# The three products of two units, woven on TensorE so that neighbours write different PSUM banks

## The reference

```python
# attention, 32 features, no softmax
scores = (xn @ q_w) @ (xn @ k_w).T * decay_weights      # strictly causal
attn = (scores @ (xn @ v_w)) @ o_w.T * out_scale
# four experts, the two best of each token mixed by a softmax of the router's logits
e0 = silu(xn @ sw_w1) * (xn @ sw_w3) @ sw_w2            # 128 -> 512 -> 128
e1 = gelu(sym(xn) @ me_c1w + me_c1b) @ me_c2w + me_c2b  # 128 -> 256 -> 128
h2 = layer_norm(syn + attn_of_syn)                      # linear maps of xn
e2 = layer_norm(h2 + relu(h2 @ f1w + f1b) @ f2w + f2b) @ gen_w + gen_b
e3 = gelu(xn @ ml_w1 + ml_b1) @ ml_w2 + ml_b2           # 128 -> 512 -> 128
```

## Time and profile before

| | |
|---|---|
| median of 3 runs | 501.11 us (500.59 to 501.36) |
| profiled execution | 500.6 us, span 498.8 us |
| PE busy | 484.0 us (97%), 3138 matmuls |
| weight loads busy | 425.3 us (85%) |
| DVE busy | 389.7 us (78%) |
| ACT busy | 224.7 us (45%) |
| POOL busy | 172.3 us (35%) |
| mean granted TensorE clock | 0.997 of full speed |

### The profile page before, as it was taken

The page is one execution under the profiler, slowest core; times in us unless marked ns, Lnnn a source line. Parts: engine busy times, 40 slices in busy tenths (PEclk is TensorE's granted clock), DMA queues, the critical chain, the costliest instruction groups (busy, mean ns, idle before and its releaser), DMA issues.

```text
span 498.8 us, 9722 instructions
## 1 busy us (share of the span) xinstructions
PE 484.0 (97%) x3138; PEld 425.3 (85%) x3138; DVE 389.7 (78%) x1310; ACT 224.7 (45%) x403; POOL 172.3 (35%) x307
## 2 busy tenths in 40 slices
PE   5899999999999999999999999999999999999995
PEld 3779898988989898898989989898898989889894
DVE  4696878779687887868789697878969788795875
ACT  3742717255262734616364361725526272452621
POOL 4642325344142433415243241524324243340320
PEclk9999999999999999999999999999999999999998
DMA  8300010000101001010100101010010100100000
GB/s 259 14 20 4 1 44 1 20 24 1 43 0 42 0 0 42 0 42 0 42 0 0 42 0 42 0 31 11 0 42 0 42 0 2 40 2 22 2 21 21
DMA packets 18497, 11.47 MB, mean 23 GB/s; under 512 B 944, under 2 KB 17840, under 8 KB 18480
## 3 DMA queue, kind: packets, MB, share of 16 engines
q1 hardware_dynamic: 18192, 11.25, 8.5%
q10 hardware_dynamic: 288, 0.01, 0.0%
HBM read 6.80 MB, written 4.19 MB: 22 GB/s over the span
## 4 chain that ended last, share of the span: by engine, by line
PE 94%; DVE 3%; DMA 1%; ACT 1%; issue 1%; POOLq 0%; DVEq 0%; POOL 0%
PE EX L904 23%; PE S L938 12%; PE S L940 11%; PE S L939 11%; PE ATT L997 7%; PE EX L916 6%; PE EX L924 3%; PE S L979 2%; PE S L947 2%; PE TR L865 2%; PE S L949 2%; PE S L948 2%; PE S L1016 2%; PE S L1018 2%; PE S L1017 1%; PE TR L976 1%
## 5 line engine op out<-in xcount | busy, mean ns | idle before, releaser
L938 PE MATMUL S<-xh,WH 128*128 128x512 f32 x224 | 94.1, 420 | 0.0
L940 PE MATMUL S<-xh,WL 128*128 128x512 f32 x224 | 88.3, 394 | 0.0
L939 PE MATMUL S<-xl,WH 128*128 128x512 f32 x224 | 88.3, 394 | 0.0
L904 PEld LDWEIGHTS EX<-W,hid 128*128 128x128 f32 x512 | 59.6, 191 | 1.4
L904 PE MATMUL EX<-scaled,hid 128*128 128x128 f32 x512 | 59.8, 275 | 0.0
L904 PE MATMUL EX<-W,hid 128*128 128x128 f32 x512 | 59.7, 274 | 0.0
L410 POOL TENSOR_TENSOR hidl<-hid,hidh 128x512 fp32r<-128x512 f32 x32 | 40.6, 1292 | 52.9 <-ACT hidh L511 52.9
L904 PEld LDWEIGHTS EX<-scaled,hid 128*128 128x128 f32 x512 | 58.5, 192 | 0.1
L374 POOL TENSOR_TENSOR veps_x<-mv_x,eps 128x4 f32<-128x4 f32 x16 | 3.2, 201 | 156.3 <-DVE mv_x L542 156.3
L652 DVE SCALAR_TENSOR_TENSOR OUT<-EX,coef,OUT 128x128 f32<-128x128 f32 x192 | 53.7, 342 | 1.3 <-PE EX L916 0.2
L938 PEld LDWEIGHTS S<-xh,WH 128*128 128x128 f32 x224 | 42.2, 188 | 14.7 <-DVE gate L728 4.6
(11 more groups left out here) (158 smaller groups left out, 963.5 us busy)
## 6 DMA issues: line engine op xcount, KB each, us to landing
X<-x SPq DMA_DIRECT2D x16, 256.0 KB, 2.9
out<-OUT SPq DMA_DIRECT2D x16, 256.0 KB, 2.4
W<-weights SPq DMA_DIRECT2D x1, 768.0 KB, 8.2
W<-weights SPq DMA_DIRECT2D x1, 512.0 KB, 5.8
W<-weights SPq DMA_DIRECT2D x1, 384.5 KB, 6.8
W<-weights SPq DMA_DIRECT2D x1, 384.0 KB, 6.3
mask<-falling SPq DMA_DIRECT2D x1, 256.0 KB, 11.7
W<-weights SPq DMA_DIRECT2D x1, 192.5 KB, 4.6
```

The lines of the kernel that those rows point to most:

```text
L904: ins = pe.matmul(EX[EX_BANK[e]][:, t, :], hid[e][:, j, t * P:(t + 1) * P], weight[:, j * P:(j + 1) * P], start=(e == 0 and j == 0), stop= ...
L938: pe.matmul(bank[:, :], wh, hi, start=True, stop=False)
L939: pe.matmul(bank[:, :], wh, lo, start=False, stop=False)
L940: pe.matmul(bank[:, :], wl, hi, start=False, stop=True).then_inc(unit_ready, 1)
```

## The change

The helper `three` for one unit is replaced by `pair` for two. It asks for both banks first, then does the six matmuls by turns, one into each bank. Every use of `three` is changed: a and b of each gate, c0 with c1, c2 with c3, f1_0 with f1_1, m0 with m1. The other engines' code is as it was.

```diff
-                def three(name, col, hi, lo):
-
-                    bank = fill(name)
-                    wh, wl = WH[:, col:col + P], WL[:, col:col + P]
-                    pe.matmul(bank[:, :], wh, hi, start=True, stop=False)
-                    pe.matmul(bank[:, :], wh, lo, start=False, stop=False)
-                    pe.matmul(bank[:, :], wl, hi, start=False, stop=True).then_inc(unit_ready, 1)
+                def pair(first_name, first_col, second_name, second_col, hi, lo):
+
+                    one, two = fill(first_name), fill(second_name)
+                    one_h, one_l = WH[:, first_col:first_col + P], WL[:, first_col:first_col + P]
+                    two_h, two_l = WH[:, second_col:second_col + P], WL[:, second_col:second_col + P]
+                    pe.matmul(one[:, :], one_h, hi, start=True, stop=False)
+                    pe.matmul(two[:, :], two_h, hi, start=True, stop=False)
+                    pe.matmul(one[:, :], one_h, lo, start=False, stop=False)
+                    pe.matmul(two[:, :], two_h, lo, start=False, stop=False)
+                    pe.matmul(one[:, :], one_l, hi, start=False, stop=True).then_inc(unit_ready, 1)
+                    pe.matmul(two[:, :], two_l, hi, start=False, stop=True).then_inc(unit_ready, 1)
...
                 def gates(j):
-                    three(f"a{j}", SPLIT["w1"] + j * P, h, l)
-                    three(f"b{j}", SPLIT["w3"] + j * P, h, l)
+                    pair(f"a{j}", SPLIT["w1"] + j * P, f"b{j}", SPLIT["w3"] + j * P, h, l)
...
-                for j in range(4):
-                    three(f"c{j}", SPLIT["ml"] + j * P, h, l)
+                for j in (0, 2):
+                    pair(f"c{j}", SPLIT["ml"] + j * P, f"c{j + 1}", SPLIT["ml"] + (j + 1) * P, h, l)
...
-                three("f1_0", SPLIT["f1"], h2h[:, :], h2l[:, :])
-                three("f1_1", SPLIT["f1"] + P, h2h[:, :], h2l[:, :])
+                pair("f1_0", SPLIT["f1"], "f1_1", SPLIT["f1"] + P, h2h[:, :], h2l[:, :])
...
-                three("m0", SPLIT["me"], h, l)
-                three("m1", SPLIT["me"] + P, h, l)
+                pair("m0", SPLIT["me"], "m1", SPLIT["me"] + P, h, l)
```

## The result

The changed kernel takes 520.2 us (519.5 to 520.9 in 4 runs) against 501.2 us: 1.0376 times as long, with a 95% interval of 1.0361 to 1.0390. The forecast was 519.4 us.

The account below looks back on a forecast made before the run. PE was taken to bound the kernel, with 94% of the span. The terms summed as 500.6 + 16.2 + 1.5 + 0.45 + 0.38 = 519.1 us, 519.6 by the median; 519.4 was given, range 511 to 523.

Parts of the forecast that it names:

- Weaving at nothing: All woven pairs on PE: removing 512 same-bank successions gains 0 us, at most 9.7 us.
- B: Rival, all woven pairs: weaving pays on the 512 successions, 509.4 us; chance 0.04.
- C: Rival, woven pairs: 19 ns saved wherever the last two predecessors filled one bank, 14.6 us, giving 498.8 us; chance 0.04.
- +0.70 for b0's bank: At c2 and c3: both begin behind b0's bank, so sc0 comes 0.70 us later in a group.
- +1.08 with sc2 and sc3 behind their Gelus: At sc2 and sc3: late Gelus of c2 and c3 delay them, 1.08 us a group including 0.70, 16.2 us in 15.
- Rival A: At c2 and c3: only the wait for b0's bank costs, 0.80 us a group, 513.4 us; chance 0.08.
- +0.10 at the token units: From m0, m1 to tok2, tok3: waiting for m1's bank costs net 0.10 us, 1.5 us in 15 transitions.
- The tail, +0.38: At the end, expert 1 waits for the last Gelu, which follows that of m0 by 0.61: +0.38 us.
- First group, +0.45: In the first group, sc2 waits for the Gelu of c2, as c0 completes 0.47 later: +0.45 us.
- What was put at nothing: Later a1, a2, a3 and f1_0 are covered; banks of a1, b1, f1_1, a2 to b3 are free early: no cost.
- rival D: Rival, behind PE's idle times before c2 and sc2: the clock falls to 1.2 GHz, 534 us or above; chance 0.04.
- What would show it: Profile signs: starts 0.23 apart, c2 waiting 0.8 us on L732 not L728, sc2 waiting 0.45, groups 1.2 us longer.

Follow-up runs that it names:

- the first experiment: Against the kernel before the change, twelve of sixteen units woven (all gates, c0 with c1, f1), c2, c3, m0, m1 left as they were: 502.0 us, 1.0017.
- the wait alone: Kernel before the change, order of products kept, only the wait for b0's bank moved ahead of c2: 512.6 us, 1.022.
- the woven kernel with the cover: Changed kernel with half of expert 1 of the group before (8 of 16 products) taken forward between pairs c0/c1 and c2/c3: 507.7 us, 1.014.

## Why the prediction was right

- **Weaving at nothing.** Right. Woven products start 0.23 to 0.24 us apart, and twelve woven units of sixteen change a group by 0.015 us. The rows of before spoke against B already: one start in three went to another bank and was no shorter. They could not speak against C, which the first experiment did. With B and C fell the 216 ns of the Trainium skill (TensorE: Matmul & The Clock Gate, Back-to-back issue gap), which no run here reached in any order: the shortest distance from the start of a 512-column product to the next start is 225 ns in all ten traces.
- **"No instruction is added."** Wrong, as the page shows: 116 waits are. Nearly all of them cost nothing, but the one ahead of c2 costs the 0.06 us a group that the next two points lack.
- **+0.70 for b0's bank.** Right for the wait alone (2.56 - 1.86 = 0.70). In the changed kernel it is 0.76; the 0.06 are the added wait, placed where it comes last.
- **+1.08 with sc2 and sc3 behind their Gelus.** Right in mechanism, 0.07 short: 1.15 a group measured with only this pair woven. 0.06 of it is the order of waits again. Rival A, in which ACT catches up, fell: sc2 waits 16 times.
- **+0.10 at the token units.** 0.09 measured. The tail, +0.38, shows as a wait of 0.77 where it was 0.43; of these 0.34 about 0.2 reach the end of the span.
- **First group, +0.45.** Too small up to sc3, too large in the end. From c1's last product to sc3 it is 3.88 us now and was 24.56 - 21.34 = 3.22, so 0.66: a wait was left out, c2 waits there as well. Half of that is given back before attention of group 0, which starts at 30.16 and started at 30.01: from c1's last product 9.00 us against 8.67, so 0.33.

```profile
21.16 0.40 PE L944 MATMUL S<-xh,WL 128*128 128x512 f32 x1
22.21 0.48 PE L939 MATMUL S<-xh,WH 128*128 128x512 f32 x1 [0.66 <-DVE hid L732]
...
25.04 0.48 PE L982 MATMUL S<-Q,K 96*128 96x512 f32 x1
```

- **What was put at nothing** (a1, b1, f1, a2 to b3) cost nothing: these pairs are in the first experiment.
- **The clock (rival D)** stayed where it was, with two pauses in each group: behind the pause before c2, from the second product on, the starts are 0.23 to 0.24 us apart.
- **What would show it.** All but one sign came as written. The line with L728 did not go away, it grew from 4.6 to 18.1 us. It names the releaser of the *weight load* of c2, which carries the wait for a0's bank, while the wait for b0's bank stands ahead of it on its own. The line on the matmul, with L732, is the true one. The wait of sc2, forecast at about 0.45 us, reads 0.3 on the matmul and 0.5 on its weight load.

The sum was 18.5 us on the profiled execution; the span grew by 18.8. Set against its parts: 462.59 - 444.20 = 18.4 us over the 15 groups from attention of group 0 on, where 17.7 had been put down; 0.15 ahead of them (30.16 - 30.01), where 0.45 had been; about 0.2 behind, where 0.38 had been. So the mechanism was right, and the total is closer than its terms since their errors cancel. The 0.15 also hold 0.18 us of luck, since c1's last product of the first group came that much earlier in this execution (21.16 against 21.34).

## What to carry to other kernels

In a ring of few buffers, taking two at a time means that the first to come free idles until the second is free, and that the first result is ready later; where buffers come free just in time, as here, this is paid in full, so read off the slack of each release before grouping. Before removing a supposed stall between neighbours, look for neighbours that already lack its cause: here every third start did. And where PE waits for a release, work that needs no such buffer can fill the wait: eight small products taken forward gave 0.6%.

## What the runs showed that was not expected

Where one matmul needs two semaphores, their order counts. In the changed kernel `fill` asks first for a0's bank and then for b0's. The wait asked for last becomes an instruction of its own on PE's queue, directly ahead of the weight load; the one asked for first sits on the weight load. If the bank that comes last is the one of the lone instruction, the weight load starts 0.06 us later than if it carries that wait itself. In the changed kernel the first weight load of c2 starts at 237.81, 0.11 behind the end of L732 at 237.70, and is put down to a0's bank:

```profile
237.81 0.19 PEld L939 LDWEIGHTS S<-xh,WH 128*128 128x128 f32 x1 [1.16 <-DVE gate L728]
```

In the kernel with the waits swapped it starts 0.05 behind the end of L732, at 236.41 + 0.69 = 237.10, and is put down to b0's bank. A group is 0.06 us shorter for nothing but this.

```profile
237.15 0.19 PEld L940 LDWEIGHTS S<-xh,WH 128*128 128x128 f32 x1 [1.09 <-DVE hid L732]
```

The cover also came with a small debt that was not foreseen: in the woven kernel with the cover, 0.04 us a group of the expected gain is missing. Its trace shows where. The eight products of expert 2 (L926) are followed by f1, 0.91 us from start to start in one group of the loop and 0.82 in the next:

```profile
208.03 1.06 PE L926 MATMUL EX<-gen_c,u 128*128 128x128 f32 x8
208.94 0.47 PE L941 MATMUL S<-h2h,WH 128*128 128x512 f32 x1
```

From the last product of expert 2 to f1 it is 0.14 us in groups 2, 4 and so on to 12, and 0.03 in all the others from group 1 on and in the changed kernel; 0.11 in six of the 14 groups is 0.046 a group. PE now comes to f1 when DVE has just made h2's low part (L751): it ends at 208.04 + 0.66 = 208.70, 0.24 us ahead of f1, where the changed kernel has 1.0. In those six groups this wait stands on its own ahead of two waits for banks, and the weight load starts at 208.91; in the others the weight load carries it itself. It looks like the effect of placement once more, but no run with the waits in another order was made here.
